# Node aggregation: one product of 192 columns per one-hot becomes three of 64 that add up in the same PSUM columns, in eight of nine passes

## The reference

```python
def step(feat, _):                                   # layer 0, four times
    transformed = jnp.einsum('nd,khd->knh', feat, W) + b[:, None, :]
    msgs = transformed[etypes, src]                  # 4 edge types
    a = jax.ops.segment_sum(msgs, dst, num_segments=num_nodes)
    return (_gru_cell(a, feat, w_ih, w_hh, b_ih, b_hh), None)
# layer 1, twice:  h = x + segment_sum(x[src], dst);  h = relu(h @ Wa + ba) @ Wb + bb
# layer 2:         segment_sum(h[src] * norm[:, None], dst) + b, relu, batch norm
# layer 3:         segment_sum(feat[src] * weight[:, None], dst) / deg, two linear maps
```

## Time and profile before

| | |
|---|---|
| median of 3 runs | 8799.82 us (8790.74 to 8809.77) |
| profiled execution, span | 8794.1 us |
| DVE busy | 7507.0 us (85%) |
| PE busy / PEld busy | 6528.0 us (74%) / 5377.6 us (61%) |
| POOL busy | 4947.8 us (56%) |
| ACT busy | 3712.2 us (42%) |
| DMA moved | 1569.18 MB, mean 178 GB/s |

### The profile page before, as it was taken

One profiled execution on the slowest core, in us unless ns is written; L12 is line 12 of the kernel. 1 busy time (PEld: TensorE's weight loads), 2 busy tenths in 40 slices (PEclk: granted clock), 3 DMA queues, 4 the chain that ended last, 5 costly groups with the idle time before them and its releaser, 6 DMA issues.

```text
span 8794.1 us, 224785 instructions
## 1 busy us (share of the span) xinstructions
PE 6528.0 (74%) x82141; PEld 5377.6 (61%) x82142; DVE 7507.0 (85%) x16891; ACT 3712.2 (42%) x9508; POOL 4947.8 (56%) x4223
## 2 busy tenths in 40 slices
PE   3776667588878887887777787766677777748888
PEld 2333333377767777776666676666566666627777
DVE  8999998699989998998988778777699978859998
ACT  1444444444445554555777533311133322234443
POOL 2555544355545556664444477588777757744443
PEclk7889998799999999998888888887799989969999
DMA  3211111377778888887766788888888888848887
GB/s 88 76 55 62 54 55 62 94 198 193 195 204 203 203 211 207 203 203 202 170 168 169 194 228 237 239 223 225 230 215 210 215 222 239 233 120 218 217 217 183
DMA packets 1157475, 1569.18 MB, mean 178 GB/s; under 512 B 407396, under 2 KB 850695, under 8 KB 1153466
## 3 DMA queue, kind: packets, MB, share of 16 engines
q1 hardware_dynamic: 916698, 898.54, 40.1%
q10 hardware_dynamic: 126656, 482.46, 16.6%
q0 software_dynamic: 113056, 174.29, 11.0%
HBM read 990.67 MB, written 564.09 MB: 177 GB/s over the span
## 4 chain that ended last, share of the span: by engine, by line
DVE 52%; DVEq 14%; DMA 11%; PE 11%; issue 8%; POOL 2%; ACT 2%; SPq 0%; ACTq 0%; POOLq 0%
DVE work L2011 7%; DVE work L1967 6%; DMA work<-bounce_f 6%; DVE work L2006 6%; DVE agg_sb L2037 4%; DVE work L1986 3%; PE ps_agg L1179 3%; DVEq L1993 3%; DMA bounce_f<-work 3%; DVE hs L1977 3%; PE ps_pair L1149 2%; POOL work L971 2%; DVE work L1788 2%; DVEq L1805 2%; DVE work L1780 2%
## 5 line engine op out<-in xcount | busy, mean ns | idle before, releaser
L971 POOL DMA_INDIRECT work<-node_rows,work x3528 | 4107.9, 1164 | 2800.8 <-DMA work<-left_recs 1396.3
L1179 PE MATMUL ps_agg<-work 120*128 120x192 bf16 x12544 | 1369.2, 262 | 446.5 <-DVE work L2011 444.4
L1149 PE MATMUL ps_pair<-rows_now,work 128*128 128x64 bf16 x39168 | 1549.5, 200 | 123.0 <-DMA work<-src_onehots 63.9
L1149 PEld LDWEIGHTS ps_pair<-rows_now,work 128*128 128x128 fp8e4 x39168 | 1468.8, 103 | 195.2 <-issue 141.7
L1179 PEld LDWEIGHTS ps_agg<-work 120*128 120x128 bf16 x12544 | 1156.3, 102 | 525.0 <-issue 495.9
L1445 ACT ACTIVATE work<-ps_pair 120x512 f32<-120x512 f32 x1632 | 954.2, 585 | 843.5 <-PE ps_pair L1149 726.6
L2006 DVE TENSOR_TENSOR work<-work 120x1024 f32<-120x1024 f32 x784 | 955.9, 1219 | 318.2 <-DMA work<-bounce_f 317.4
L1967 DVE TENSOR_TENSOR work<-iota_bf,dl_all 120x2048 bf16<-120x2048 bf16 x882 | 1079.1, 1223 | 36.8 <-SPq L739 15.3
L2011 DVE TENSOR_TENSOR work<-work 120x1024 f32<-120x1024 f32 x784 | 961.6, 1227 | 72.7 <-issue 3.0
L1201 PE MATMUL ps_agg<-work 128*128 128x192 bf16 (+1 forms) x7840 | 885.0, 257 | 165.5 <-DMA work<-node_rows,work 159.6
L1201 PEld LDWEIGHTS ps_agg<-work 128*128 128x128 bf16 x7840 | 656.7, 102 | 195.7 <-issue 148.9
(11 more groups left out here) (345 smaller groups left out, 11490.8 us busy)
## 6 DMA issues: line engine op xcount, KB each, us to landing
bounce_f<-work ACTq DMA_DIRECT2D x816, 480.0 KB
work<-bounce_f SPq DMA_DIRECT2D x784, 480.0 KB
work<-src_onehots SPq DMA_DIRECT2D x918, 256.0 KB
bounce<-work ACTq DMA_DIRECT2D x102, 727.5 KB
work<-bounce SPq DMA_DIRECT2D x98, 727.5 KB
work<-node_rows,work POOLq DMA_INDIRECT x3528
hs<-grid_vals SPq DMA_DIRECT2D x49, 960.0 KB, 5.0
node_rows<-stage SPq DMA_DIRECT2D x686, 48.0 KB
```

What stands on the lines that cost most here:

```text
L971: pool.indirect_dma_start(out=ring[:, at.slot6() * LB + b, 0:3 * H], out_offset=None, in_=table_of(at.p), in_offset=bass.IndirectOffsetOnA ...
L1149: last = mm(to[:, a * H:(a + 1) * H], oh[s.buf()][:, EIGHT * m + a, :], rows_now[:, s.chunk() * CHUNK + EIGHT * m + a, x * H:(x + 1) * H], ...
L1179: last = mm(acc[:, to:to + 3 * H], hot, tops(thirds[at.two()])[0:ROWS, :, b, :], start=b == 0 or p < P_GIN1 and b == GB // 2, stop=False)
```

## The change

In passes 0 to 7 each destination one-hot meets the three parts in three products of 64 columns, which all add into the same 64 PSUM columns of the type, where before one product of 192 columns left the three parts side by side. The count column of pass 0 moves next to them. DVE then takes 64 columns a type: one addition where there were three with two drains, and in passes 4 to 7 no reduction, the own row's scaled addition reading PSUM directly. Pass 8 and the set-up stay.

```diff
@@ grid
-                    last = mm(acc[:, to:to + 3 * H], hot, tops(thirds[at.two()])[0:ROWS, :, b, :],
-                              start=b == 0 or p < P_GIN1 and b == GB // 2, stop=False)
+                    for x in range(3):
+                        last = mm(acc[:, to:to + H], hot, tops(thirds[at.two()])[0:ROWS, x, b, :],
+                                  start=x == 0 and (b == 0 or p < P_GIN1 and b == GB // 2), stop=False)
                     if p == 0:
-                        last = mm(acc[:, to + 3 * H:to + 3 * H + 1], hot, ones_b[0:ROWS, 0:1], start=False, stop=False)
+                        last = mm(acc[:, to + H:to + H + 1], hot, ones_b[0:ROWS, 0:1], start=False, stop=False)
@@ left_over_batch
-                    n = 3 * H + (1 if p == 0 else 0)
-                    last = mm(acc[:, k * AGG:k * AGG + n], hot, ring[:, u * LB + b, 0:n], start=False,
-                              stop=end and (p >= P_GIN1 or k % 2 == 1))
+                    for x in range(3):
+                        n = H + (1 if p == 0 and x == 2 else 0)
+                        last = mm(acc[:, k * AGG:k * AGG + n], hot, ring[:, u * LB + b, x * H:x * H + n], start=False,
+                                  stop=end and x == 2 and (p >= P_GIN1 or k % 2 == 1))
@@ take_sums
-                    v.tensor_tensor(counts[...], typed[:, :, 3 * H],
+                    v.tensor_tensor(counts[...], typed[:, :, H],
                                     own_rec[:, 0:K], ALU.add)
                 dve.wait_ge(own_scaled, at.tiles(1))
-                for x in range(3):
-                    if x > 0:
-                        dve.drain()
-                    last = v.tensor_tensor(to, to, typed[:, :, x * H:(x + 1) * H], ALU.add)
+                last = v.tensor_tensor(to, to, typed[:, :, 0:H], ALU.add)
...
-                v.tensor_reduce(out=to, in_=acc[:, 0:3 * H].rearrange("p (a f) -> p f a", a=3), axis=AX.X, op=ALU.add)
-                dve.drain()
                 if p == P_SAGE:
+                    v.tensor_reduce(out=to, in_=acc[:, 0:3 * H].rearrange("p (a f) -> p f a", a=3), axis=AX.X, op=ALU.add)
+                    dve.drain()
...
                     last = v.scalar_tensor_tensor(out=to, in0=own_x[at.half()][:, :], scalar=own_rec[:, OWN_N:OWN_N + 1],
-                                                  in1=to, op0=ALU.mult, op1=ALU.add)
+                                                  in1=acc[:, 0:H], op0=ALU.mult, op1=ALU.add)
```

More of the change, by code:

```diff
@@ L2030, in take_sums @@
                 if p == 0:
-                    v.tensor_tensor(counts[:, ds(at.d(), 1), 1:K + 1].rearrange("p o k -> p (o k)"), typed[:, :, 3 * H],
+                    v.tensor_tensor(counts[:, ds(at.d(), 1), 1:K + 1].rearrange("p o k -> p (o k)"), typed[:, :, H],
                                     own_rec[:, 0:K], ALU.add)
                 dve.wait_ge(own_scaled, at.tiles(1))
-                for x in range(3):
-                    if x > 0:
-                        dve.drain()
-                    last = v.tensor_tensor(to, to, typed[:, :, x * H:(x + 1) * H], ALU.add)
+                last = v.tensor_tensor(to, to, typed[:, :, 0:H], ALU.add)
                 if p == 0 or careful:
```

## The result

The changed kernel takes 8593.89 us (median of four, 8581 to 8638) against 8804.80 for the kernel before, timed beside it: a ratio of 0.977, with an interval of 0.9747 to 0.9792. That is 211 us less. The forecast was 8430 us, so the sign was right and the time lies inside the range, but little more than half of the 373 us came.

A forecast was written before the change was run, and what follows sets the result against it. VectorE was taken to bound passes 0 to 3 and 6; savings of 203 (passes 0 to 2), 90 (3), 36 (6), 39 (4 and 7) and 5 us (5), together 373, took 8794 to 8421, given as 8430; range 8290 to 8620.

The forecast's parts named there:

- Bound: Passes 0 to 3 and 6 belong to VectorE; passes 4, 5 and 7 are shared with the gathers and DMA.
- VectorE's 0.99 and 0.43 us: VectorE saves 0.99 us a typed tile from two additions, 0.43 us in passes 4 to 7 from the reduction and drain.
- TensorE's pace: Products of 64 columns run at 29 to 30.5 ns; TensorE needs 0.16 us more a typed tile, 0.11 in passes 4 to 7.
- the rival of the weight load: TensorE's bf16 weight load sets the pace at 83 ns a product, 4.2 us more a typed tile: 11050 us, chance 0.06.
- What comes late next: In passes 0 to 2 the DMA engines' load holds the tile at 6.85 us, between 6.59 and 7.1: 203 us saved.
- The prediction's own sign of being wrong: Typed tiles staying over 7.2 us, or passes 4 to 7 moving by more than 150 us in all.
- Passes 3 and 6: Pass 3 saves 0.92 us a tile, 90 us; pass 6, owned by VectorE, saves 0.37 us a tile, 36 us.
- Passes 4, 5 and 7: Passes 4 and 7, partly DMA, save 0.2 us a tile, 39 us together; pass 5, POOL and gathers, 5 us.
- the sign that was named for the DMA rival: Waits of over 100 us a pass for `bounce_f` would mean that DMA took the saving back.
- DMA takes it back: A DMA ceiling of 0.87 keeps typed tiles at 7.1 us, nothing in passes 4, 5, 7: 8566 us, chance 0.20.
- the four: Rivals: DMA ceiling 8566 us, 0.20; VectorE's saving in full 8255, 0.08; weight load 11050, 0.06; nothing moved 8800, 0.04.

The follow-up runs named there:

- VectorE's part alone: Kernel before with one addition for three and no reduction in passes 4 to 7, products unchanged, middle and low parts left out: 8444 us.
- the longer products' run: VectorE's saving without the split products, plus eight unread products of 62 columns a tile in passes 0 to 3: 8459 us.
- The new order: Changed kernel with the second half of the octet's work moved ahead of the first products in passes 0 to 3: 8556 us.

## Why the prediction was right, and where its sum was not

*Bound.* Right. Typed passes belonged to VectorE: with its work cut and nothing else, they went from 7.54 to 6.80 us a tile.

*VectorE's 0.99 and 0.43 us.* Right in the typed passes: L2036 is one of 0.41 us a tile, and undisturbed tiles recur after 6.6 to 6.8 us where 6.55 was the floor. In pass 4 it is not seen (691 to 688, and 696 with VectorE's part alone).

*TensorE's pace.* Right, and with it the rival of the weight load fell: bf16 loads with 64 columns run at 30 ns, (1.61 - 0.2) / 47, well below the 40 at which the change would have lost. From group start to group start the cost is 0.14 + 0.08 = 0.22 us a tile (1.47 and 1.45, against 1.33 in the earlier trace rows and 1.37 for an unhindered grid in the run with VectorE's part alone), where 0.16 was set. By the longer products' run, that is worth some 15 us. The Trainium skill's pair of load and product at 81 ns ("TensorE: Matmul & The Clock Gate", "Back-to-back issue gap") is stated for 128 columns. The run with two products a one-hot has that size and does not bear it out: with its own load each, the next product starts 55 to 58 ns after one of 128 columns.

*What comes late next.* This is the step that failed. It asked of every engine and queue whether it could keep the new pace, and found the DMA's bytes; it did not ask it of the instructions. I had counted the added products by their time, 0.16 us, and not as 128 instructions, for which two thirds as many pages again have to come (74 to 122 in pass 1). The value that it took, 6.85 us a tile for passes 0 to 2, was nevertheless what VectorE's part alone gives (6.85, 6.80 and 6.79), at a DMA share of 0.88. That this came so near is luck, since no floor of DMA, from which 6.85 was taken, showed there. In the changed kernel the term was mis-sized: 0.69 us a tile became 0.23, 0.37 and 0.37, or, by the passes' lengths, 86 us for 203, and the instructions took the difference. The loss has two parts that the traces show and no run here separates: the holes themselves, and the lower clock that follows some of them. (The new order keeps the holes and loses most of the falls in pass 1, but it also gives TensorE room.) That the time still lies inside the range is luck in part, too: the forecast's own range ended at 8540, and what lies above was there for DMA. The prediction's own sign of being wrong, typed tiles over 7.2 us, was missed closely in passes 1 and 2 (7.17 and 7.16) and met in pass 0 (7.65).

*Passes 3 and 6.* Right in pass 6, 37 us for 36, and nearly so in pass 3: 77 for 90, 836 us for the 820 to 830 named. TensorE had 1.19 us of waiting in a tile of pass 3, and its 31 holes with 22 us cost little there: 829 us with VectorE's part alone.

*Passes 4, 5 and 7.* 3, 12 and -19 us in the profile, where 20, 5 and 20 were forecast: 49 us less, of which pass 7 is 39. VectorE's wait for `bounce_f` grew in pass 7 (47 to 81 us in 500 us of it), the sign that was named for the DMA rival, though short of its 100 us. This rival's own place, passes 0 to 2, was not where it decided: in pass 1 that wait is 16.2 us, where it was 10.4 before.

*The rivals.* "DMA takes it back" came closest by its time (8566), for a wrong reason. None of the four had the mechanism that decided. The Trainium skill has a rule on it: "Runtime: NRT & Kernel Launch", section "Instruction fetch mechanics", says that instructions come in blocks of 16 KiB, 256 each, which agrees with the 259 to a packet of 16.4 KB above but for 1%, and that an engine fetches the next block while it executes the one before, at a cost that is "mostly hidden". In the kernel before this holds: no "issue" stands in front of its grid in pass 1. In the changed kernel it doesn't: there are 31.6 us.

## What to carry to other kernels

When a change splits one instruction into several, count instructions as a resource of their own: take the instruction queue's packets before, scale them by the new count, and divide the time of the pass by them. Here 7.2 us a page cost nothing, 6.0 us cost half of a gain and 6.25 cost little, because another engine left room. A gap in the middle of a group of like products, with "issue" as its releaser, is the mark; the median of a tile hides it and the mean shows it. Where it can't be avoided, move independent work into a wait that TensorE has anyway, so that a late page finds room.

## What the runs showed of the hardware

- TensorE runs 144 pairs of load and product in a row at some 30 ns a pair, so 15 ns an instruction, and in some tiles it stopped in them for up to 2.3 us until 1.2 to 1.6 us after a page's landing.
- A weight load that no product uses is nearly free in time (four to a product of 192 columns: 0.10 us a tile for 128 of them) and such loads still cost 149 us on 8444, of which the time they take explains no more than 15; their pages are the rest.
- The granted clock fell to 1.2 GHz some 2 us after a hole of 0.92 us, for 3.4 us, in a pass where it had been at 2.4 GHz for 618 us on end in the kernel before (0.99 over pass 1, 0.96 after). In tiles 8 to 90 of pass 1 it did not fall at all with VectorE's part alone or with the longer products, once in the kernel before, and six times in the changed kernel.
